# Edge weights reordered and half of them scaled on the way out of PSUM, the one-hot of a pair in one instruction, and the second layer's radial product over 96 rows

## The reference, cut to what matters

```
h = relu(layernorm(x));  x = x + h + feats(layer 0 of h)
h = relu(layernorm(x));  x = x + layer 1 of h

per edge:  w  = act(edge_embed @ fc1) @ fc2          # 192 weights: ss 64, sv 64, vs 32, vv 32
           xs, xv = (s @ W_s)[src], (v @ W_v)[src]
           m0_a = w_ss * xs * sh0                    # 64
           m0_b = w_vv * sum_c(xv_c * sh1_c) / sqrt(3)   # 32
           m1_a = w_sv * xs * sh1_c                  # 3 x 64
           m1_b = w_vs * xv_c * sh0                  # 3 x 32
agg = segment_sum([m0_a, m0_b, m1_a, m1_b], dst);  out = agg @ W2 (+ self product, gates in layer 0)
```

## Time and profile before

| | us |
|---|---|
| median of 3 runs | 2910.91 |
| lowest, highest | 2899.09, 2930.3 |
| profiled execution, its own time | 2901.78 |
| its span, first to last instruction | 2900.0 |
| busy PE / PEld / DVE | 2652.8 / 2448.7 / 2546.0 |
| busy ACT / POOL | 2101.9 / 1783.5 |
| mean granted TensorE clock | 0.97 |

### The profile page before, as it was taken

How to read it: one execution, slowest core, us unless ns; L and a number is a source line. 1 busy time by engine, 2 the same in 40 slices (tenths; PEclk the granted TensorE clock), 3 DMA queues, 4 the chain that set the end, 5 groups by cost and what they waited for, 6 DMA issues and landing times. The chain is left out here.

```text
span 2900.0 us, 93514 instructions
## 1 busy us (share of the span) xinstructions
PE 2652.8 (91%) x26822; PEld 2448.7 (84%) x26822; DVE 2546.0 (88%) x11404; ACT 2101.9 (72%) x5020; POOL 1783.5 (61%) x2035
## 2 busy tenths in 40 slices
PE   0699999999999999999999995799999999999997
PEld 0699999999999999999999994688888888888886
DVE  6799999999999999999999992587888888788886
ACT  1599999999999999999999994354455555444453
POOL 3677766776666677766676661555566555555651
PEclk9999999999999999999999997799999999899998
DMA  5244444444444444444444431455555555455552
GB/s 133 71 108 112 110 111 110 111 111 112 111 108 110 108 114 111 110 112 111 110 111 108 110 100 51 105 144 129 132 146 141 147 142 141 125 141 136 140 140 74
DMA packets 563778, 337.76 MB, mean 116 GB/s; under 512 B 220529, under 2 KB 545684, under 8 KB 563141
## 3 DMA queue, kind: packets, MB, share of 16 engines
q1 hardware_dynamic: 462033, 216.02, 29.4%
q0 software_dynamic: 48736, 83.76, 11.6%
q10 hardware_dynamic: 52500, 32.01, 3.8%
HBM read 199.48 MB, written 132.08 MB: 114 GB/s over the span
## 5 line engine op out<-in xcount | busy, mean ns | idle before, releaser
L677 POOL DMA_INDIRECT xg<-sources,win x501 | 583.8, 1165 | 489.8 <-issue 221.0
L677 POOL DMA_INDIRECT xg<-in_x,win x501 | 611.2, 1220 | 164.8 <-issue 153.2
L1140 PE MATMUL out_ps<-w_out,aggT 128*100 128x64 f32 (+2 forms) x6012 | 635.6, 256 | 9.5 <-issue 6.9
L1140 PEld LDWEIGHTS out_ps<-w_out,aggT 128*100 128x100 f32 x6012 | 607.3, 171 | 12.2 <-issue 7.5
L1128 PE MATMUL agg_ps<-sel,msg 128*128 128x100 f32 x4512 | 594.8, 282 | 6.7 <-DVE msg L824 4.5
L1128 PEld LDWEIGHTS agg_ps<-sel,msg 128*128 128x128 f32 x4512 | 544.2, 195 | 26.3 <-DVE msg L824 5.5
L967 ACT COPY xw_sb<-xw_ps 128x704 f32<-128x704 f32 (+1 forms) x502 | 307.0, 611 | 315.5 <-PE xw_ps L1116 154.0
L1116 PE MATMUL xw_ps<-w_fc,hid 65*128 65x192 f32 (+1 forms) x2004 | 461.2, 354 | 17.9 <-ACT hid L942 13.4
L986 ACT COPY aggT<-agg_ps 128x600 f32<-128x600 f32 x377 | 248.2, 658 | 150.7 <-PE agg_ps L1128 91.0
L1116 PEld LDWEIGHTS xw_ps<-w_fc,hid 65*128 65x128 f32 (+1 forms) x2004 | 322.4, 194 | 33.7 <-ACT hid L942 17.6
L950 ACT ACTIVATE hn<-xn,nmr,rs 128x192 f32<-128x192 f32 x501 | 244.4, 538 | 56.5 <-DVE nmr L772 56.5
(11 more groups left out here) (147 smaller groups left out, 5488.8 us busy)
## 6 DMA issues: line engine op xcount, KB each, us to landing
sources<-ev SPq DMA_DIRECT2D x250, 250.0 KB
xn<-in_x SPq DMA_DIRECT2D x250, 125.0 KB
xmid<-xo SPq DMA_DIRECT2D x250, 125.0 KB
xo<-xmid SPq DMA_DIRECT2D x250, 125.0 KB
xn<-sources SPq DMA_DIRECT2D x250, 125.0 KB
out<-xo ACTq DMA_DIRECT2D x250, 125.0 KB
win<-edge_rec SPq DMA_DIRECT2D x1002, 3.5 KB
ee_sb<-ee_parts SPq DMA_DIRECT2D x501, 18.0 KB
```

The lines of the kernel that those rows point to most:

```text
L677: pool.indirect_dma_start(out=xg[:, t.slot, j, 0:D], out_offset=None, in_=edge_rows, in_offset=bass.IndirectOffsetOnAxis(ap=win[:, t.slot, ...
L1140: ins = pe.matmul(rows[0:NT, j, c0:c1], aggT[:, t.half, j, k, :], w[f"out{k}_"][:, :], start=fresh, stop=True, skip_group_check=not fresh)
```

## The change

- The 192 columns of `fc2` are reordered from ss, sv, vs, vv to sv, vv, ss, vs (`by_use`).
- ACT copies the node products, sv and vv plainly (2 x 256 columns in the first layer, 2 x 96 in the second), and then scales the 96 weights ss and vs by sh0 while it copies them out of PSUM, one instruction for each tile. `xs0` is gone, and L818 and L821 multiply the plain node products by the scaled weights.
- The semaphore of the scaled copies, `scaled_ready`, takes the place of `xs0_ready`, and PE's `radial` (first layer) and `edges` now wait for it instead of `xw_copied`.
- The one-hot of a pair becomes one `scalar_tensor_tensor` over 2 x 100 columns with the tile's offset as a constant; `base` and `move_base` (L793) go, except in the second pass.
- The second layer's radial product contracts over 96 rows: `fc1_1` gets 86 rows of zeros, and `ee_sb` is 96 partitions tall, of which the DMA fills the first 10. What lies in the others is finite and is multiplied by zero.

```diff
@@ -38,6 +38,7 @@
 SW = MUL0 + MUL1
 BLOCKS = 4 * SW // P
 WN = 2 * MUL0 + 2 * MUL1
+W_SV, W_VV, W_SS, W_VS = 0, MUL0, SW, SW + MUL0
 NT = 100
 TILES = N // NT
 PAIR = 2
...
@@ -151,7 +152,7 @@
         starts = sb("starts", [1, LISTED], I32)
 
 
-        ee_sb = sb("ee_sb", [PARTS * PARTS * nf + PARTS, S1, PAIR, 2 * P], BF16)
+        ee_sb = sb("ee_sb", [SW, S1, PAIR, 2 * P], BF16)
         xg = sb("xg", [P, S1, PAIR, XW])
         xn = sb("xn", [P, S1, PAIR, XW])
         xo = sb("xo", [P, S1, PAIR, XW])
...
@@ -486,7 +488,7 @@
     deep = 1 if first else 2
     edge_rec, long_tab, long_num, ee = v["edge_rec"], v["long_tab"], v["long_num"], v["ee_parts"] if layer == 0 else v["ee"][1]
     nrow = ee.shape[0]
-    krad = PARTS * nrow + PARTS if first else nrow
+    krad = PARTS * nrow + PARTS if first else SW
     ee_all = ee_sb[:, :, :, 0:P] if first else ee_sb[:, :, :, :].bitcast(F32)
     fc1 = v["fc1_parts"] if first else w["fc1_"]
     hidden = 64 if first else 100
...
@@ -407,9 +408,10 @@
                 dve.wait_ge(s_cast, g + 1)
                 dve.tensor_tensor(e_buf[:, :, :], e_buf[:, :, :], e_parts[:, g * nf:(g + 1) * nf, :], ALU.subtract).then_inc(s_rest, 1)
             for name, scale in (("fc2_0", 1.0), ("fc2_1", np.sqrt(2.0) / np.sqrt(100.0))):
-                a = WN - MUL1
-                dve.tensor_scalar(w[name][:, 0:a], w[name][:, 0:a], float(scale), None, ALU.mult)
-                dve.tensor_scalar(w[name][:, a:WN], w[name][:, a:WN], float(scale * r3), None, ALU.mult)
+                dve.tensor_scalar(w[name][:, :], w[name][:, :], float(scale), None, ALU.mult).then_inc(s_fc2, 1)
+            for k, name in enumerate(("fc2_0", "fc2_1")):
+                dve.wait_ge(s_fc2, k + 1)
+                dve.tensor_scalar(w[name][:, W_VV:W_SS], w[name][:, W_VV:W_SS], float(r3), None, ALU.mult)
 
             dve.wait_ge(s_found, 16 * 2 * TC)
             for k in range(2 * TC):
...
@@ -780,17 +782,16 @@
 
                 b = t.tiles
                 dve.wait_ge(win_in[t.slot], (t.uses + 1) * (32 * b))
-                dve.wait_ge(base_set, t.m + 2 if t.serial else t.n + 1)
                 hold(dve, agg_done, t.freed(2))
-                for j in range(b):
-                    ins = dve.tensor_scalar(sel[:, t.half, j, :], iota_n[:, :], win[:, t.slot, j, 1:2].bitcast(F32), base[:, j:j + 1],
+                if t.serial:
+                    dve.wait_ge(base_set, t.m - (NB - 1))
+                    ins = dve.tensor_scalar(sel[:, t.half, 0, :], iota_n[:, 0, :], win[:, t.slot, 0, 1:2].bitcast(F32), base[:, 0:1],
                                             ALU.subtract, ALU.is_equal)
+                else:
+                    rows = win[:, t.slot, 0:b, 1:2].bitcast(F32).to_broadcast([P, b, NT])
+                    ins = dve.scalar_tensor_tensor(out=sel[:, t.half, 0:b, :], in0=iota_n[:, 0:b, :], scalar=float(t.n * PAIR * NT), in1=rows,
+                                                   op0=ALU.add, op1=ALU.is_equal)
                 ins.then_inc(sel_ready, 1)
-
-            def move_base(t):
-
-                dve.wait_ge(sel_ready, t.n + 1)
-                dve.tensor_scalar(base[:, :], base[:, :], -float(PAIR * NT), None, ALU.add).then_inc(base_set, 1)
 
             def messages(t):
                 b = t.tiles
...
@@ -803,10 +804,9 @@
                 else:
                     dve.wait_ge(xg_in[t.slot], (t.uses + 1) * (16 * b))
                     dve.wait_ge(win_in[t.slot], (t.uses + 1) * (32 * b))
-                x1 = xs0[:, t.half, 0:b, :]
                 wt = xw_sb[:, t.half, 0:b, D:D + WN]
                 e1 = harmonics(t)[:, :, 1:4].unsqueeze(3)
-                dve.tensor_tensor(pw[:, 0:b, :], x_s, wt[:, :, MUL0:2 * MUL0], ALU.mult).then_inc(pw_ready, 1)
+                dve.tensor_tensor(pw[:, 0:b, :], x_s, wt[:, :, W_SV:W_VV], ALU.mult).then_inc(pw_ready, 1)
                 dve.tensor_tensor(qv[:, 0:b, :, :], x_v, e1.to_broadcast([P, b, 3, MUL1]), ALU.mult).then_inc(qv_ready, 1)
                 hold(dve, agg_done, t.freed(2))
                 dve.wait_ge(pw_ready, t.n + 1)
@@ -814,14 +814,14 @@
                                   e1.to_broadcast([P, b, 3, MUL0]), ALU.mult)
                 dve.wait_ge(qv_ready, t.n + 1)
                 dve.tensor_tensor(tv[:, 0, 0:b, :], qv[:, 0:b, 0, :], qv[:, 0:b, 1, :], ALU.add).then_inc(tv_ready, 1)
-                dve.wait_ge(xs0_ready, t.n + 1)
-                dve.tensor_tensor(msg[:, t.half, 0:b, 0, 0:MUL0], x1[:, :, 0:MUL0], wt[:, :, 0:MUL0], ALU.mult)
+                dve.wait_ge(scaled_ready, t.n + 1)
+                dve.tensor_tensor(msg[:, t.half, 0:b, 0, 0:MUL0], x_s, wt[:, :, W_SS:W_VS], ALU.mult)
                 dve.wait_ge(tv_ready, t.n * 2 + 1)
                 dve.tensor_tensor(tv[:, 1, 0:b, :], tv[:, 0, 0:b, :], qv[:, 0:b, 2, :], ALU.add).then_inc(tv_ready, 1)
-                dve.tensor_tensor(msg[:, t.half, 0:b, 1:4, MUL0:SW], x1[:, :, MUL0:D].rearrange("p j (c m) -> p j c m", c=3),
-                                  wt[:, :, 2 * MUL0:2 * MUL0 + MUL1].unsqueeze(2).to_broadcast([P, b, 3, MUL1]), ALU.mult)
+                dve.tensor_tensor(msg[:, t.half, 0:b, 1:4, MUL0:SW], x_v,
+                                  wt[:, :, W_VS:WN].unsqueeze(2).to_broadcast([P, b, 3, MUL1]), ALU.mult)
                 dve.wait_ge(tv_ready, t.n * 2 + 2)
-                dve.tensor_tensor(msg[:, t.half, 0:b, 0, MUL0:SW], tv[:, 1, 0:b, :], wt[:, :, WN - MUL1:WN],
+                dve.tensor_tensor(msg[:, t.half, 0:b, 0, MUL0:SW], tv[:, 1, 0:b, :], wt[:, :, W_VV:W_SS],
                                   ALU.mult).then_inc(msg_ready, 1)
 
             def gated_vectors(t):
...
@@ -884,8 +881,6 @@
                     new_rows(t)
                     if first:
                         stats2(t)
-                if t := T(4):
-                    move_base(t)
                 if t := T(3):
                     messages(t)
                 if (t := T(6)) and first:
...
@@ -963,18 +958,16 @@
                 b = t.tiles
                 act.wait_ge(xw_done, t.n + 1)
                 hold(act, msg_ready, t.freed(2))
-                c = 0 if first else D
-                act.copy(xw_sb[:, t.half, 0:b, c:xw], w_ps[:, 0:b, :]).then_inc(xw_copied, 1)
-                if first:
-                    act.wait_ge(xw_copied, t.n + 1)
+                if first:
+                    act.copy(xw_sb[:, t.half, 0:b, 0:D + W_SS], xw_ps[:, 0:b, 0:D + W_SS]).then_inc(xw_copied, 1)
                     act.wait_ge(she_ready, t.n + 1)
                 else:
-                    act.wait_ge(xg_in[t.slot], (t.uses + 1) * (16 * b))
+                    act.copy(xw_sb[:, t.half, 0:b, D:D + W_SS], w_ps[:, 0:b, 0:W_SS]).then_inc(xw_copied, 1)
                     act.wait_ge(win_in[t.slot], (t.uses + 1) * (32 * b))
                 for j in range(b):
-                    xs = xw_sb[:, t.half, j, 0:D] if first else xg[:, t.slot, j, 0:D]
-                    ins = act.activation(xs0[:, t.half, j, :], xs, ACT.Copy, scale=harmonics(t)[:, j, 0:1])
-                ins.then_inc(xs0_ready, 1)
+                    ins = act.activation(xw_sb[:, t.half, j, D + W_SS:D + WN], w_ps[:, j, xw - SW:xw] if first else w_ps[:, j, W_SS:WN],
+                                         ACT.Copy, scale=harmonics(t)[:, j, 0:1])
+                ins.then_inc(scaled_ready, 1)
 
             def copy_agg(t):
                 b = t.tiles
...
@@ -1093,7 +1086,7 @@
 
                 pe.wait_ge(win_in[t.slot], (t.uses + 1) * (32 * t.tiles))
                 if first:
-                    hold(pe, xw_copied, t.freed(1))
+                    hold(pe, scaled_ready, t.freed(1))
                 hold(pe, hid_ready, t.freed(1))
                 for j in range(t.tiles):
                     ins = pe.matmul(hid_ps[0:fc1.shape[1], j, :], fc1[:, :], ee_all[0:krad, t.slot, j, :],
@@ -1264,6 +1257,17 @@
             t[(c + 1) * SW:(c + 2) * SW, outw + c * MUL1:outw + (c + 1) * MUL1] = vectors
         return {f"out{k}_{layer}": t[k * P:(k + 1) * P, c0:c1] for k, (c0, c1) in enumerate(out_cols(outw))}
 
+    def by_use(m):
+
+        ss, sv, vs, vv = np.split(m, np.cumsum([MUL0, MUL0, MUL1]), axis=1)
+        return np.concatenate([sv, vv, ss, vs], axis=1)
+
+    def below(m):
+
+        t = np.zeros((SW, m.shape[1]), np.float32)
+        t[:m.shape[0]] = m
+        return t
+
     def beside(m):
 
...
@@ -1277,11 +1281,11 @@
     g1 = {k[7:]: v for k, v in a.items() if k.startswith("L1_gnn_")}
     weights = {
         "fc1_0": beside(np.concatenate([g0["fc_w1"], g0["fc_b1"][None]], axis=0)),
-        "fc2_0": np.concatenate([g0["fc_w2"], g0["fc_b2"][None]], axis=0),
+        "fc2_0": by_use(np.concatenate([g0["fc_w2"], g0["fc_b2"][None]], axis=0)),
         "lin0": halves([g0["W1_s"]], [g0["W1_v"]]),
         "sc0": halves([gates_first(g0["Wsc_s"])], [g0["Wsc_v"]]),
         **out_blocks(0, gates_first(g0["W2_s"]), g0["W2_v"]),
-        "fc1_1": g1["W_fc1"], "fc2_1": g1["W_fc2"],
```

(15 more changed lines are left out.)

4 lines of the change are left out of this document (1 added, 3 removed).

## The result

| us | before | changed |
|---|---|---|
| median of 4 runs | 2905.0 | 3000.26 |
| lowest, highest | 2884.29, 2930.3 | 2986.27, 3007.95 |
| profiled execution, its own time | 2901.78 | 3007.95 |
| its span | 2900.0 | 3006.2 |

The ratio is 1.0347, with a 95% interval from 1.0269 to 1.0425; it leaves out the kernel before's run of 2930.3, a slow one by being over 1.5% above its fastest. The forecast was 2884, its range ended at 2942.

The account below looks back on a forecast made before the run. PE's loop with ACT was taken to bound the first layer, PE the second. From 2901.8 us, -85 + 8 + 55 gave 2880 for the profiled execution, and 4 more for the median 2884 us; range 2820 to 2942.

Parts of the forecast that it names:

- Rows, -85 us: Second layer's radial product: 96 rows instead of 10 remove a bubble on PE, 0.34 us a step, 85 us less in all.
- Rival 5: Second layer's radial product: the bubble stays, by the count of columns or another cause; 2969 us, chance 0.07.
- The new wait, +55: First layer: PE's radial product now waits for both scaled copies on ACT; 0.22 us a step, 55 us more in all.
- The loop: First layer: from L1099's load through PE's work and ACT's copies back to that load; forecast 6.85 us, 0.24 over 6.61.
- What the prediction said of L1158: First layer, as a sign: PE would idle before L1099's load, and no longer mainly before L1158.
- Rivals 1, 3 and 4: 1: new wait hides, 2829 us, 0.16; 3: DVE sets first layer's pace, 2767, 0.03; 4: wait costs upper bound, 2954, 0.13.
- DVE's relief as cover: Second layer: DVE's work falls from 3.49 to 3.24 us a step, which lets PE have its 0.34.
- Stalls of the second layer, +8: Second layer: 23 stalls stay, but each loses 0.34 us of slack that absorbs its beginning; 8 us more.
- Rival 2 (clock stays up): Second layer: the clock stays up since PE streams more densely, 36 us less; 2848 us, chance 0.12.

## Why the prediction was wrong, by its steps

**Rows, -85 us: right.** Measured 90 (ten rows against 96, calm); 0.362 a step. The Trainium skill's rule by which rows would not matter (TensorE: Matmul & The Clock Gate, LDWEIGHTS) would have made this 0, and these runs are against it for the step as a whole. The page says it of a load's duration, and there the trace is near it: 163 ns on the mean with 10 rows, 177 with 96. Rival 5 is out. That few rows drain PE is the prediction's reading; what the runs show is that the bubble goes with the rows.

**The new wait, +55: right in kind, too large.** Measured 39. The loop closed as described; the changed kernel:

```profile
1012.39 0.59 ACT L962 COPY xw_sb<-xw_ps 128x512 f32<-128x512 f32 x1
...
1012.87 0.58 ACT L968 ACTIVATE xw_sb<-xw_ps,she 128x96 f32<-128x96 f32 x2
...
1013.52 0.16 PEld L1092 LDWEIGHTS xw_ps<-ee_sb,fc_parts 75*96 75x96 bf16 x2
```

From the copy's start to the end of the scaled copies it is 1.06 us (1.10 forecast), 0.07 more to the load (0.09). The two errors of 0.04 and 0.02, and 0.01 elsewhere, are most of the difference between 0.22 and 0.15 a step. What the prediction said of L1158 was wrong: PE still waits there for L1016 (it was L1023), 176 times, 37.8 us, beside the new wait. Rivals 1, 3 and 4 are out: the scaled copy took 0.346, the wait 0.15 a step and not 0.50, and the first layer's step grew while DVE's work shrank.

**DVE's relief as cover: right.** Without it the step is 3.55, with it 3.49.

**Stalls of the second layer, +8: this step failed.** Calm, the changed kernel takes 2771 against 2822, and these 51 us are what -90 and +39 make. In the disturbed condition, in which it was measured, the stalls took 256 us in place of 98: +158, where the prediction had +8. With -90 and +38 (0.151 a step) that makes +106, and the profiled executions differ by 106.2. The step priced each of 23 stalls by the slack that it loses, as if their number and length came from outside. In the traces they come with runs of gathers, and the change turned runs of mostly one or two into runs of up to eleven. The prediction had POOL's "2.36 a step" and left it at that; it never asked what held a gather for 1.63 us when another took 0.95. It listed the one-hot among DVE's savings, 0.33 twice becoming 0.41, and did not look at which operands the new instruction reads, nor who waits for that. It had DVE's own step fall below PE's and took that for cover alone; it is also the pace at which gathers are held. None of the rivals had a place for it. Rival 2 (clock stays up) went the other way when disturbed: 0.90. Calm, it is 1.00 from 2000 to 2500 us. The calm time, 2771, lies outside the range as well, below it: the forecast started from a time with the disturbance's stalls in it.

What stays open: what the disturbed condition is (the DMA packets took about as long in both: a gather's 4480-byte packets 0.27 and 0.30 us on the mean in the two disturbed profiles of the changed kernel, 0.28 in the calm one), why a run of gathers slows PE there alone, and what starts the first stall of a circle.

## What to carry to other kernels

When two DVE operations become one, look at the operands, not just at the time: an operation with a single tensor input may be the opening through which GpSimd's software DMAs get their turn, and what counts is how many of them fit into one step, at DVE's own pace too and not only at the pace that another engine sets. A mean duration far above the shortest one of the same instruction (1.17 against 0.95 us here) is a sign of being held. And a stall that has no price in the trace should be followed to what starts it before it is carried over unchanged; run the kernel before on more than one chip, for the sign may turn with the condition: this change is 1.8% faster in one and 3.5% slower in the other.
